# The position MLP of a two-layer attention kernel, taken in pairs of units

## What is computed

```
pos = qgrid[None, :, None, :] - kvgrid[:, None, :, :]
bias = jnp.sign(pos) * jnp.log1p(jnp.abs(pos))
bias = jax.nn.relu(bias @ cpb_w1.T + cpb_b1)
bias = jax.nn.relu(bias @ cpb_w2.T + cpb_b2)
bias = bias @ cpb_w3.T + cpb_b3
sim = sim + bias.reshape(B, HEADS, H * W, Hp * Wp)
```

## Time and profile before

| | us |
|---|---|
| median of 3 runs | 3876.17 |
| lowest, highest | 3869.98, 3879.89 |
| the profiled execution, its own time | 3866.95 |
| its span, first to last instruction | 3865.0 |

### The profile page before, as it was taken

One profiled execution on the slowest core, in us unless ns is written; L12 is line 12 of the kernel. 1 busy time (PEld: TensorE's weight loads), 2 busy tenths in 40 slices (PEclk: granted clock), 3 DMA queues, 4 the chain that ended last, 5 costly groups with the idle time before them and its releaser, 6 DMA issues.

```text
span 3865.0 us, 48290 instructions
## 1 busy us (share of the span) xinstructions
PE 3495.5 (90%) x19360; PEld 2006.9 (52%) x19360; DVE 2227.1 (58%) x2923; ACT 1602.7 (41%) x2296; POOL 221.3 (6%) x165
## 2 busy tenths in 40 slices
PE   5989799899988999889998999989998999996978
PEld 2554456455554456544555445654465554563444
DVE  3554566466564665555655656547565575663764
ACT  0441444263442534334443535416354163452633
POOL 0000020000100010000200002000020000200200
PEclk9999899999999999999999999999999999998989
DMA  2011001300013000120002200021001210003020
GB/s 70 9 31 60 3 13 31 94 12 27 13 31 92 12 27 15 48 74 17 23 15 67 53 28 17 15 72 42 33 13 31 77 31 24 13 11 93 12 62 33
DMA packets 129423, 139.64 MB, mean 36 GB/s; under 512 B 78993, under 2 KB 98964, under 8 KB 128532
## 3 DMA queue, kind: packets, MB, share of 16 engines
q1 hardware_dynamic: 129204, 136.56, 12.9%
HBM read 99.48 MB, written 37.03 MB: 35 GB/s over the span
## 4 chain that ended last, share of the span: by engine, by line
PE 75%; DMA 8%; DVE 7%; issue 4%; ACT 4%; SPq 1%; POOL 0%; DVEq 0%; ACTq 0%; POOLq 0%
PE banks L477 14%; PE banks L512 11%; PE banks L527 10%; PE banks L496 9%; PE banks L540 8%; PE banks L676 4%; PE banks L558 3%; DMA x_dram<-exps 3%; PE banks L686 3%; PE banks L677 3%; PE banks L678 3%; DMA recips_dram<-recips 3%; PE banks L665 2%; DMA x_image<-in_x 2%; PE banks L655 1%
## 5 line engine op out<-in xcount | busy, mean ns | idle before, releaser
L1107 DVE TENSOR_REDUCE neg_max<-banks 128x1 f32<-128x1024 f32 x512 | 602.5, 1218 | 264.6 <-PE banks L496 258.0
L866 ACT ACTIVATE exps<-banks,neg_max 128x1024 f32<-128x1024 f32 x512 | 564.6, 1111 | 208.6 <-DVE neg_max L1107 208.4
L512 PE MATMUL banks<-ident,exps 128*128 128x128 f32 x4096 | 567.6, 282 | 70.1 <-DVE exps_turned L1116 50.3
L876 ACT ACTIVATE exps_turned<-banks 128x1024 f32<-128x1024 f32 x256 | 262.0, 1024 | 822.0 <-PE banks L512 821.3
L512 PEld LDWEIGHTS banks<-ident,exps 128*128 128x128 f32 x4096 | 448.9, 143 | 249.1 <-issue 249.1
L527 PE MATMUL banks<-exps_turned,values 128*64 128x256 f32 x4096 | 508.4, 392 | 13.1 <-issue 6.8
L496 PE MATMUL banks<-qk_halves 64*128 64x512 f32 x3072 | 428.2, 410 | 85.1 <-ACT exps L866 41.1
L1116 DVE COPY exps_turned<-banks 128x1024 f32<-128x1024 f32 x256 | 313.0, 1223 | 248.3 <-PE banks L512 247.5
L496 PEld LDWEIGHTS banks<-qk_halves 64*128 64x128 f32 x3072 | 281.5, 186 | 280.7 <-issue 243.0
L1273 DVE SCALAR_TENSOR_TENSOR qk_halves<-banks,qk_halves 128x1024 fp32r<-128x1024 f32 x256 | 312.0, 1221 | 140.8 <-ACT qk_halves L913 139.2
L527 PEld LDWEIGHTS banks<-exps_turned,values 128*64 128x64 f32 x4096 | 280.1, 139 | 171.5 <-issue 65.2
(11 more groups left out here) (153 smaller groups left out, 3215.8 us busy)
## 6 DMA issues: line engine op xcount, KB each, us to landing
x_image<-in_x SPq DMA_DIRECT2D x8, 2048.0 KB, 9.2
recips_b<-recips_dram SPq DMA_DIRECT2D x256, 64.0 KB, 3.7
exps_turned<-in_x SPq DMA_DIRECT2D x32, 512.0 KB, 7.8
x_dram<-exps SPq DMA_DIRECT2D x32, 512.0 KB, 2.6
exps_turned<-x_dram SPq DMA_DIRECT2D x32, 512.0 KB, 19.7
out<-exps_turned SPq DMA_DIRECT2D x32, 512.0 KB, 2.6
attended<-mlp_rows SPq DMA_DIRECT2D x96, 112.0 KB
exps_turned<-in_wo SPq DMA_DIRECT2D x8, 1024.0 KB, 5.5
```

The source lines that it names most:

```text
L512: mm = pe.transpose(TB[:, kt // 4, kt % 4 * P:kt % 4 * P + P], PB[:, 2 * h + n % 2, kt * P:(kt + 1) * P], IDENT[:])
L866: freed(act.activation(PB[:, 2 * h + n % 2], slot(("s", m, i)), ACT.Exp, bias=NM[:, m:m + 1], accum_out=SS[:, m:m + 1]), ("s", m, i))
L1107: dve.tensor_reduce(NM[:, m:m + 1], slot(("s", m, i)), AX.X, ALU.max, negate=True).then_inc(mx, 1)
```

## The change

The first layer is issued for both units of a window together: one block of four matmuls, on all four row groups, after a wait for both ring slots. High and low halves get four buffers each: `h1_hi_half(u)` and `h1_lo_half(u)` take the tensor's other half too, by `u // 2 % 2`, and `relu1(u)` waits for the products of unit `u - 4`. ScalarE and VectorE do the first-layer work of both units of the next pair, then the second-layer work of both units of this one. On TensorE `mlp3(v - 1)` stands between the third and the fourth product group of pair `v`; before, it stood behind the fourth and the block that followed. The number of matmuls and their shapes stay as they were.

```
--- before.py
+++ after.py
@@ -127,8 +127,6 @@
 
 
         X2 = PB
-        H1H = QK[:, 1, 0:2]
-        H1L = QK[:, 1, 2:4]
         H2 = PB
         AT = PB
         PT_LO = PT[:, 0].rearrange("p h t q -> p (h t q)")
@@ -316,6 +314,12 @@
         def x2_loads(j):
             return 16 * (min(j + 2, B) + j + 1)
 
+        def h1_hi_half(u):
+            return QK[:, u // 2 % 2, u % 2]
+
+        def h1_lo_half(u):
+            return QK[:, u // 2 % 2, 2 + u % 2]
+
         def h2_bank(c):
             return (TB[:, 0], TB[:, 1], MB)[c % 3]
 
@@ -657,26 +661,28 @@
                     filled(mm, ("lq", t, i))
 
             def mlp(j):
-                def mlp1(u):
-                    wait_free(pe, ("h1", u, j))
-                    for w in range(2):
-                        s = 2 * (u % 2) + w
+                def mlp1(v):
+                    for u in (2 * v, 2 * v + 1):
+                        wait_free(pe, ("h1", u, j))
+                    for s in range(4):
+                        u, w = 2 * v + s // 2, s % 2
                         rows = slice(32 * s, 32 * s + 3 * ROWS)
                         mm = pe.matmul(slot(("h1", u, j))[:, 512 * w:512 * w + 512], W1R[rows],
-                                       RR[rows, C * (u // 2):C * (u // 2) + C],
-                                       start=True, stop=True)
-                    filled(mm, ("h1", u, j))
-
-                def mlp2(u):
-                    wait_emptied(pe, ("h1", u, j))
-                    for w in range(2):
-                        c = 2 * u + w
-                        if c >= 3:
-                            pe.wait_ge(h2_done[(c - 3) % 2], j * UNITS + (c - 3) // 2 + 1)
-                        pe.matmul(h2_bank(c), W2H[:], H1H[:, u % 2, 512 * w:512 * w + 512], start=True, stop=False)
-                        pe.matmul(h2_bank(c), W2H[:], H1L[:, u % 2, 512 * w:512 * w + 512], start=False, stop=False)
-                        pe.matmul(h2_bank(c), W2L[:], H1H[:, u % 2, 512 * w:512 * w + 512], start=False, stop=True)\
-                            .then_inc(h2_full[w], 1)
+                                       RR[rows, C * v:C * v + C], start=True, stop=True)
+                        if w:
+                            filled(mm, ("h1", u, j))
+
+                def mlp2(u, w):
+                    c = 2 * u + w
+                    if w == 0:
+                        wait_emptied(pe, ("h1", u, j))
+                    if c >= 3:
+                        pe.wait_ge(h2_done[(c - 3) % 2], j * UNITS + (c - 3) // 2 + 1)
+                    cols = slice(512 * w, 512 * w + 512)
+                    pe.matmul(h2_bank(c), W2H[:], h1_hi_half(u)[:, cols], start=True, stop=False)
+                    pe.matmul(h2_bank(c), W2H[:], h1_lo_half(u)[:, cols], start=False, stop=False)
+                    pe.matmul(h2_bank(c), W2L[:], h1_hi_half(u)[:, cols], start=False, stop=True)\
+                        .then_inc(h2_full[w], 1)
 
                 def mlp3(v):
 
@@ -690,13 +696,19 @@
 
                 pe.wait_ge(rows_in, (j + 1) * 192)
                 mlp1(0)
+                mlp2(0, 0)
+                mlp2(0, 1)
                 mlp1(1)
-                for u in range(UNITS):
-                    mlp2(u)
-                    if u + 2 < UNITS:
-                        mlp1(u + 2)
-                    if u % 2 and u >= 3:
-                        mlp3(u // 2 - 1)
+                mlp2(1, 0)
+                mlp2(1, 1)
+                for v in range(1, WIN):
+                    if v + 1 < WIN:
+                        mlp1(v + 1)
+                    mlp2(2 * v, 0)
+                    mlp2(2 * v, 1)
+                    mlp2(2 * v + 1, 0)
+                    mlp3(v - 1)
+                    mlp2(2 * v + 1, 1)
                 mlp3(WIN - 1)
 
             def turn_bias(j):
@@ -908,15 +920,17 @@
             def mlp(j, i):
                 def relu1(u):
                     wait_full(act, ("h1", u, j))
-                    if u >= 2:
-                        act.wait_ge(h2_full[1], j * UNITS + u - 1)
-                    act.activation(H1H[:, u % 2], slot(("h1", u, j)), ACT.Relu).then_inc(h1_hi, 1)
+                    if u >= 4:
+                        act.wait_ge(h2_full[1], j * UNITS + u - 3)
+                    act.activation(h1_hi_half(u), slot(("h1", u, j)), ACT.Relu).then_inc(h1_hi, 1)
 
                 act.wait_ge(x2_out, 64 * min(j + 2, B))
                 relu1(0)
+                relu1(1)
                 for u in range(UNITS):
-                    if u + 1 < UNITS:
-                        relu1(u + 1)
+                    if u % 2 == 0 and u + 2 < UNITS:
+                        relu1(u + 2)
+                        relu1(u + 3)
                     act.wait_ge(h2_full[0], j * UNITS + u + 1)
                     if u >= 4:
                         act.wait_ge(l3_done, j * WIN + u // 2 - 1)
@@ -1270,15 +1284,17 @@
             def mlp(j, i):
                 def low1(u):
                     dve.wait_ge(h1_hi, j * UNITS + u + 1)
-                    freed(dve.scalar_tensor_tensor(out=H1L[:, u % 2], in0=slot(("h1", u, j)), scalar=0.0,
-                                                   in1=H1H[:, u % 2].bitcast(F32), op0=ALU.max, op1=ALU.subtract),
+                    freed(dve.scalar_tensor_tensor(out=h1_lo_half(u), in0=slot(("h1", u, j)), scalar=0.0,
+                                                   in1=h1_hi_half(u).bitcast(F32), op0=ALU.max, op1=ALU.subtract),
                           ("h1", u, j))
 
                 low1(0)
+                low1(1)
                 dve.wait_ge(x2_out, 64 * min(j + 2, B))
                 for u in range(UNITS):
-                    if u + 1 < UNITS:
-                        low1(u + 1)
+                    if u % 2 == 0 and u + 2 < UNITS:
+                        low1(u + 2)
+                        low1(u + 3)
                     dve.wait_ge(h2_full[1], j * UNITS + u + 1)
                     if u >= 4:
                         dve.wait_ge(l3_done, j * WIN + u // 2 - 1)
```

## The result

The changed kernel took 3863.19 us (median of 20 runs, 3850.27 to 3875.61), the kernel before 3874.63 us (median of 20, 3859.06 to 3880.59). The ratio is 0.9973, with a 95% interval of 0.9964 to 0.9982: 10.5 us less, 7 to 14. Two later sets, in which the kernel before took 3857 and 3859 us, gave the same kernel 0.9968 (0.9955 to 0.9980) and 0.9978 (0.9968 to 0.9989). So it is faster, by about 60% of the 18 us that were forecast. The gain of 0.27% is clear of noise only because 20 runs of each stand behind it: the prediction had called everything within 0.3% no change that can be measured, and had given that outcome 0.23, against 0.70 for more. The profiled execution has a span of 3864.0 us. Single executions of one kernel differ by 20 us and more, so what follows compares the stretches of the MLP inside a profile, and ratios of medians for the time.

A forecast was written before the change was run, and what follows sets the result against it. The MLP was taken as bound by TensorE's issue. Per stretch 5.0 - 0.8 - 0.5 - 1.1 = 2.6 us less; the eight stretches fall from 663.2 to 645.4, 18 us less, giving 3858 us, range 3845 to 3872.

The forecast's parts named there:

- rival B: Start of each stretch: the new wait keeps TensorE's clock low 10 us more, 35 us in all, 3893; chance 0.07.
- The block of four: First layer on TensorE: four matmuls take 0.32 us at full clock, as two do; saves 5.0 us a stretch.
- Rival C: First-layer block: the four matmuls do not run together, 0.64 us a block, 28 us more in all, 3886; chance 0.05.
- The plain pair: Pair of units without row statistics on TensorE: 4.50 us instead of 4.83, with nothing in it a wait.
- The cover by the third layer: Third layer ahead of the fourth product group: ScalarE's bank is ready 0.65 us early; otherwise a wait of 0.4.
- Item 3: End of each stretch: the last third layer waits 0.9 us for VectorE, plus a 0.2 break; 1.1 us given back.
- Item 1: Start of each stretch: fourth product group waits 1.25 us for ScalarE, an old 0.47 wait goes; net 0.8 given back.
- The 80.9 us of the forecast: Each of the seven MLP stretches with row statistics: 80.9 us expected, from 83.5 in the stretch followed.
- Item 2: Four pairs with row statistics, in seven stretches: VectorE needs 4.78 us, over 4.50; net 0.5 us a stretch given back.
- Rival A: Statistics pairs: VectorE instructions do not overlap, 5.3 us a pair, 14 us given back, 3872; chance 0.14.

The follow-up runs named there:

- behind: Changed kernel with the third layer behind the fourth product group in every pair, not between third and fourth: 3880.61 us, ratio 1.0061 to the kernel before.
- tail: Changed kernel, but in each stretch's last pair the third layer of the pair before stands behind the fourth product group: 3848.26 us, ratio 0.9976.
- fill: Changed kernel with two dummy matmuls on TensorE between third and fourth product group, at the start of each stretch only: 3847.96 us, ratio 0.9972.
- start: Changed kernel with unit 0's second-layer ReLUs ahead of the first-layer work of units 2 and 3, on ScalarE and VectorE: 3845.78 us, ratio 0.9969.
- warm: Changed kernel with dummy matmuls at each start, 14 before the wait for the rows and 10 before the first product: 3843.33 us, ratio 0.9965.
- start_tail: Changed kernel with the edits of start and tail together: 3841.60 us, ratio 0.9954.
- start_tail2: The kernel of start_tail run a second time: 3837.75 us, ratio 0.9950.
- all: Changed kernel with the edits of start and tail and the dummy matmuls of warm: 3834.22 us, ratio 0.9938.
- best: As all, with the dummy matmuls left out of the last stretch: 3823.26 us, ratio 0.9914 to the kernel before.
- before_warm: The kernel before the change with the same dummy matmuls as warm: 3855.20 us, ratio 0.9998.

## Why the forecast was right, and where it was off

The direction, the saving in the pair and the range held: forecast 18 us less, 3858 in a range of 3845 to 3872; measured 10.5 less, 3863.19. The size did not: the gain lies inside the 0.3% that the prediction would have called no change, and one of its own signs of being wrong stood in the profile, a granted clock of 0.50 beyond some 10 us from a start (B), in all eight stretches. By its steps:

- **The block of four costs what a block of two costs**: 0.32 us at full clock, measured 0.32. Rival C is excluded.
- **The plain pair** at 4.50 us: 4.51 measured, in the pairs without statistics up to the last two. The cover by the third layer is real: without it 4.89 (behind), and a kernel slower than before.
- **Item 3, the end**: a wait of 0.9, measured 0.94; the end in all 1.1, measured 1.15 (tail).
- **Item 1, the start**, is the term that was mis-sized. The wait itself was forecast at 1.25 and is 1.02, or 1.5 to 1.7 where the clock had risen. The 80.9 us of the forecast leave 13.7 up to the first third layer. The prediction held that the clock could only help ("The new start hangs on the ReLU queues and hardly gains"), and its sum took for granted that it rises no later than before. It does: the low time at the start ends at 14.9 us on average instead of 8.3, and the first third layer came at 15.2 (14.5 and 14.6 in the other two profiles). The term was 0.8 us net a stretch and measured 2.3 (1.6 in the others), 7 to 12 us in all. That was rival B's mechanism at a part of its price: some 5 us more at the low level, where the price of B (44%) would make it 2.3 us a stretch and 0.8 to 1.5 were measured. That this is the reason for the missing part of the time is argued from the stretches only: fill took the second fall away, and its ratio did not move.
- **Item 2, the statistics pairs**: 4.78 us each for VectorE is right (4.77 in fill). But in the changed kernel only the last of them reaches it, since the slow start lets VectorE catch up. I had the two as independent terms that add; they share one queue, and the larger hides the smaller. Where the start is fast, four pairs reach 4.76 and not three, so the item was held too small for that case: the part behind the first third layer then takes 67.9 us instead of 67.2. For the 1.13 us between two low halves the prediction shows no row (the earlier trace rows has 1.15); 1.13 is what the new order has (2.26 for the two at 1702.23).
- Rival A: VectorE's starts are 4.77 us a pair, not 5.3, in the new order too, so in these rows an operation does begin before the one ahead has ended. The rule of the Trainium skill ("VectorE: DVE Perf Modes", section "The DRAIN you can't avoid") that the prediction set beside it is given there with an exception which the prediction left out: a next operation that is not held back starts earlier. These rows agree with the exception, with 0.65 us from start to start behind an operation of 0.74 us.
- The Trainium skill ("TensorE: Matmul & The Clock Gate", section "A second HAM failure mode: psum-queue depth-cycling") has short idle times between groups that rotate through PSUM banks make the clock swing. The traces agree in part: at the start the clock fell again behind a wait of 1.5 to 1.7 us in three of eight stretches. They do not in the steady pairs: in behind, with a wait of 0.3 us in every pair, the clock was low only at the starts.

**What stays open.** In every variant of the changed kernel with shorter stretches the time fell by less than they did. Against the changed kernel (three profiles, 655 to 659 us in the stretches; three ratios, 0.9973 on average; a difference of 0.001 is 3.9 us of time):

| run | stretches, us less | time, us less |
|---|---|---|
| tail | 9 to 14 | 0 |
| start | 9 to 13 | 2 |
| fill | 6 to 10 | 0 |
| warm | 16 to 21 | 3 |
| start_tail, start_tail2 | 19 to 26 | 7 to 9 |
| all | 31 to 35 | 14 |
| best | 30 to 34 | 23 |

In warm and all the dummies ahead of the last stretch explain 5 us of it. before_warm has 16 and 1 against the kernel before. The first profile of the changed kernel is off the other way: its stretches fell by 4 us and its time by 10.5. One profile for each kernel, whose rest of the span varies by 10 us and more between executions of the same kernel (3191.6 to 3204.8 for the changed one), cannot say where it goes. Whether it is given back elsewhere, or whether these profiled executions were merely good ones, was not settled. Those of tail, start, warm and fill were 3 to 7 us below the medians of their runs, which speaks for a part of the second; that of start_tail was 4 above. So the second fall of the clock is shown as the cause of what the stretches lack at their start, and not as the cause of the 7 us that the time lacks.

## What to carry to other kernels

Work an order change on several engines through engine by engine, with start-to-start times from the trace: here it gave pair, cover and tail to within 0.1 us. Then look at the ramps separately, since a new order shows its waits where the queues are still empty, and a wait of 1 us there brought the first third layer 1.2 to 1.8 us later through the matrix engine's clock (15.2, 14.5 and 14.6 against 13.4 in fill), though 0.7 us of that was caught up later and the time shows none of it. And what a filler instruction covers (the third layer ahead of the fourth group) can decide the sign: the same pairing without it was 0.6% slower than no pairing.

## What the hardware showed that I had not expected

- The clock that rose 7 us behind a start went back to 0.50 behind a time in which TensorE was busy for 1.69 of 3.40 us, while in the kernel before it rose once in each start and did not fall again. In start_tail2 it stayed at 1.00 through 1.53 of 3.50 us. Two matmuls that compute nothing, put into that wait, kept it up in eight of eight stretches, though they filled only a part of it.
- A block of four matmuls on four row groups takes the same 0.32 us at full clock as one of two on two.
- Matmuls of constants in place of idle time (24 in each of seven stretches) were a net gain together with the other two edits: ratio 0.9914 for best against 0.9950 and 0.9954 for the edits alone. Alone (warm 0.9965, before_warm 0.9998) they gave nothing that stands clear of the intervals.
